# Plain TensorE products that nobody reads, in the score stage and the norms of a decoder layer

## The reference

```python
q, k, v = heads(x @ Wq), heads(x @ Wk), heads(x @ Wv)
attn = softmax(q @ k.T / sqrt(D))
...
x = layernorm(x + ((1 - blend) * attn @ v + blend * splat_attention(q, k, v)) @ Wo)
...
x_dbl = einsum('ke,bel->bkl', x_proj_w, u)
delta = softplus(einsum('er,brl->bel', dt_proj_w, dt_lo) + dt_proj_b)
state = state * exp(d_t * A) + (d_t * u_t) * B_t      # 512 steps, 512 x 16 states
x = layernorm(x + (y * silu(x)))
...
gate, up = split(x @ ternary(w_gate_up))
x = layernorm(x + rms_norm(silu(gate) * up) @ ternary(w_proj))
```

## Time and profile before

| | |
|---|---|
| median of 3 runs | 1458.05 us (1455.8 to 1459.01) |
| the profiled execution | 1459.91 us, its span from first to last instruction 1458.2 us |
| mean granted TensorE clock | 0.872 of full speed |
| busy | PE 83%, DVE 83%, ACT 52%, POOL 11% |
| the chain that ended last | PE 40%, DVE 35%, issue 9%, ACT 4% |

### The profile page before, as it was taken

How to read it: one execution, slowest core, us unless ns; L and a number is a source line. 1 busy time by engine, 2 the same in 40 slices (tenths; PEclk the granted TensorE clock), 3 DMA queues, 4 the chain that set the end, 5 groups by cost and what they waited for, 6 DMA issues and landing times.

```text
span 1458.2 us, 14219 instructions
## 1 busy us (share of the span) xinstructions
PE 1212.7 (83%) x4693; PEld 556.5 (38%) x4698; DVE 1204.1 (83%) x1457; ACT 763.8 (52%) x1118; POOL 164.9 (11%) x211
## 2 busy tenths in 40 slices
PE   4563885788689989899899898889799898987996
PEld 3332322233245543333355443333355433323553
DVE  5878898889979998879889997889799998786223
ACT  6765543536367753537477653455677545352331
POOL 1000111001101120100101121001111211001001
PEclk9875885889869999779889998799899998788998
DMA  6853796466329959553259686362389595540231
GB/s 196 286 170 116 169 248 165 102 145 145 59 87 244 253 133 265 132 129 87 67 135 271 165 226 192 87 166 52 89 220 269 120 255 133 135 104 15 65 102 44
DMA packets 112666, 220.20 MB, mean 151 GB/s; under 512 B 14560, under 2 KB 25312, under 8 KB 112592
## 3 DMA queue, kind: packets, MB, share of 16 engines
q1 hardware_dynamic: 88608, 142.85, 32.1%
q0 software_dynamic: 18432, 67.12, 23.9%
q10 hardware_dynamic: 5552, 9.31, 1.8%
HBM read 122.37 MB, written 29.62 MB: 104 GB/s over the span
## 4 chain that ended last, share of the span: by engine, by line
PE 40%; DVE 35%; issue 9%; ACT 4%; DMA 1%; DVEq 0%; POOL 0%; ACTq 0%; POOLq 0%
DVE ST L904 12%; PE ps L1382 6%; PE ps L1321 5%; PE ps L1514 5%; DVE MX L960 5%; PE ps L1304 5%; DVE ST L896 5%; PE ps L1458 3%; PE ps L1379 3%; PE ps L1414 3%; PE ps L1474 3%; DVE QAK L1130 2%; DVE QS L1117 2%; DMA YA<-ST 1%; DVE BST L940 1%
## 5 line engine op out<-in xcount | busy, mean ns | idle before, releaser
L904 DVE TENSOR_TENSOR_SCAN ST<-dA,ST 128x1024 f32<-128x1024 f32 x128 | 293.0, 2289 | 12.9 <-ACT dA L593 10.3
L1514 PE MATMUL ps<-V,GU 128*128 128x512 f16 x1024 | 239.9, 390 | 5.6 <-DVE V L1104 5.6
L960 DVE TENSOR_REDUCE MX<-ps 128x1 f32<-128x512 f32 x256 | 165.2, 686 | 76.3 <-PE ps L1304 76.0
L509 POOL DMA_DIRECT2D YA<-ST x128 | 109.3, 854 | 980.4 <-DVE ST L907 914.7
L593 ACT ACTIVATE dA<-DL,Aneg 128x511 f32<-128x511 f32 x256 | 168.3, 713 | 63.4 <-DVE ST L904 59.1
L731 ACT ACTIVATE PT<-ps 128x1024 f32<-128x1024 f32 x128 | 127.0, 1021 | 122.9 <-PE ps L1414 122.2
L1304 PE MATMUL ps<-KS,QS 96*128 96x512 f32 x256 | 129.4, 571 | 50.9 <-DVE MX L960 44.0
L907 DVE TENSOR_TENSOR ST<-ST,BC 128x1024 f32<-128x1024 f32 x128 | 156.8, 1225 | 4.4
L896 DVE TENSOR_TENSOR ST<-DU,BC 128x1024 f32<-128x1024 f32 x128 | 155.9, 1218 | 0.4 <-DMA YA<-ST 0.4
L1514 PEld LDWEIGHTS ps<-V,GU 128*128 128x128 bf16 x1024 | 97.4, 100 | 142.1 <-issue 33.0
L1474 PE MATMUL ps<-QS 128*128 128x512 f32 x512 | 142.1, 421 | 2.5 <-DVE QS L1117 1.6
(11 more groups left out here) (231 smaller groups left out, 1530.3 us busy)
## 6 DMA issues: line engine op xcount, KB each, us to landing
YA<-ST POOLq DMA_DIRECT2D x128, 512.0 KB, 7.3
BC<-bc_rows SPq DMA_DIRECT2D x64, 512.0 KB, 7.6
GU<-gu_tiles SPq DMA_DIRECT2D x64, 256.0 KB, 4.8
QS<-proj_tiles SPq DMA_DIRECT2D x64, 256.0 KB, 4.2
QS<-qk_parts SPq DMA_DIRECT2D x32, 256.0 KB, 4.2
KS<-qk_parts SPq DMA_DIRECT2D x32, 256.0 KB, 5.5
ST<-in_L_ffn_w_gate_up_dram SPq DMA_DIRECT2D x16, 256.0 KB, 3.7
gu_tiles<-BC SPq DMA_DIRECT2D x16, 256.0 KB, 2.1
```

What stands on the lines that cost most here:

```text
L904: nc.vector.tensor_tensor_scan(flat, dA[:, a, :, :].rearrange("p e s -> p (e s)"), flat, 0.0, ALU.mult, ALU.add).then_inc(s_scan, 1)
L960: nc.vector.tensor_reduce(MX[:, j % 2, qt, h:h + 1], ps[:, n % 2, :], AX_X, ALU.max).then_inc(s_mx, 1)
L1514: last = mm(ps[:, f % F_RING, :], GU[:, t % GU_RING, k, m * P:(m + 1) * P], XHL[:, z, k, :], start=(k == 0 and z == 0), stop=(k == KT - 1 ...
```

## The change

A new function `keep_busy(bank, times)` issues plain fp32 products of the identity matrix by one slice of `W`, into a PSUM bank whose content is not read any more. Nothing reads their results, and no semaphore is raised by them. The order of the instructions has 71 of them: 18 in each of batches 0 to 2, and 17 in the last.

- Score stage, ten a batch: one before and one behind the transposes of the first group's maxima; in group 1 three between the first two and the last two of the four `max_scores` that follow its first four L1414, and two behind the next pair of L1414; in group 2 three behind that same pair.
- Norms, eight a batch: one between `prep_xd` and `prep_dt` (not in the last batch), and 2, 1, 2 and 2 around the transposes of the second layernorm's rows.
- Each place has a wait that makes its bank free: for the last copies of Q and K out of bank 6 (`s_hi`), for the first or second exponential of the group (`s_exp`), for the last reads of the dt banks (`s_abs`, `s_rel`). That last wait stood behind the second tile of the feed-forward products before.

```diff
+            def keep_busy(bank, times):
+
+                for _ in range(times):
+                    mm(ps[:, bank, :], ident[:, :], W[:, 3, 0, :], start=True, stop=True)
...
                 max_scores(b, 0, 12, 16)
+                pe.wait_ge(s_hi, 2 * NG * (b + 1))
+                keep_busy(6, 1)
                 transpose_max(b, 0)
+                keep_busy(6, 1)
                 max_scores(b, 1, 0, X_AHEAD)
...
                             last.then_inc(s_s, 1)
+                            if j == 1 and kt == 0 and p == 1:
+                                max_scores(b, j + 1, 0, 2)
+                                pe.wait_ge(s_exp, 2 * KT * NG * b + 2 * KT * j + 1)
+                                keep_busy(score_bank(b, j, 0), 3)
+                                cuts[p] = 2
+                            if 0 < j < NG - 1 and kt == 1 and p == 0:
+                                pe.wait_ge(s_exp, 2 * KT * NG * b + 2 * KT * j + 2)
+                                keep_busy(score_bank(b, j, 2), 1 + j)
                             max_scores(b, j + 1, cuts[p], cuts[p + 1])
...
                     prep_xd(b + 1)
+                    keep_busy(7, 1)
                     for e in range(KT):
                         prep_dt(b + 1, e)
...
+                if not last_batch:
+                    pe.wait_ge(s_abs, KT * (b + 2))
+                    pe.wait_ge(s_rel, KT * (b + 2))
                 for r in range(KT):
+                    if r < KT - 1:
+                        keep_busy(7, (2, 1, 2)[r])
                     pe.wait_ge(s_lnx, 3 * KT * b + KT + r + 1)
...
+                keep_busy(7, 2)
                 pe.wait_ge(s_xl, KT * (b + 1))
...
-                    if t == 1 and not last_batch:
-                        pe.wait_ge(s_abs, KT * (b + 2))
-                        pe.wait_ge(s_rel, KT * (b + 2))
```

## The result

The changed kernel takes 1444.98 us (median of 4 runs, 1444.05 to 1445.55), the one before 1458.53 in the same comparison (4 runs, 1455.8 to 1459.31). The ratio is 0.9908, with a 95% interval of 0.9895 to 0.9921: 13.5 us less. I had forecast 1429, 29 us less. The profiled execution took 1444.05 us, with a span of 1442.3; its mean granted clock is 0.912, where it was 0.872.

A forecast was written before the change was run, and what follows sets the result against it. Taken as bound: neither TensorE nor DVE alone, TensorE's half clock making DVE wait. Of 42.3 us if all held, B and C 20.3, A 5.2, D 6.2 make 31.7; less a tenth, 28.5: 1429 us, range 1415 to 1450.

The forecast's parts named there:

- B: Score stage, group 1: clock held saves 13.6 us over batches 1 to 3; nine tenths taken, with C 20.3.
- C: Score stage, group 2: clock held saves 9.0 us over batches 1 to 3; nine tenths taken, with B 20.3.
- half of it holds: Rival, 27%: in each batch one or two places fall to half clock all the same; about 14 us gained, 1444.
- A: Around the transposes of the first group's maxima: 3.5 us a batch if held, 10.5 in three; half taken, 5.2.
- Windows at 0.50 shrink to one or none: Sign: half-clock stretches in batches 1 to 3 shrink from four a batch to one or none.
- mean clock above 0.92: Sign: TensorE's mean clock over the kernel rises from 0.872 to above 0.92.
- D: Norms, with the dt products and the gate and up products behind: 8.2 us if held; three quarters taken, 6.2.
- the case in which D gives little: If transposes don't count as work for the clock, D gives 6.2 us less: 1436; some 5 in a hundred.
- The 1.0 that I had counted for the dt products: In D: batch 1's dt products take 4.67 us against 3.69 in batch 2, so 1.0 to gain.
- Where a stretch gets faster other waits appear: a tenth off: Deduction over the whole sum for new waits, such as for ACT's exponentials: 31.7 us becomes 28.5.
- the overshoots: Products outlast their waits and delay work: 0.2 us in A, 1.2 in B, 0.6 in C, at most 0.5 in D.
- the slower rival: Rival, 9%: clock falls in or ahead of the products, each then takes 1.87 us; 24 us in four batches, 1482.

The follow-up runs named there:

- no_products: Changed kernel with every product taken out, the new order and waits kept; 1459.46 us, ratio 1.0006 to the kernel before.
- a_behind: Changed kernel plus a third product in A, behind the four max_scores, in the wait for the bias row; 1433.73 us, ratio 0.9823 to the kernel before.
- a_three_only: Kernel before plus only A's three products, the third behind the four max_scores; 1445.12 us, ratio 0.9918.
- few_rows: Changed kernel with all products working on 16 of the array's 128 rows; 1503.7 us, ratio 1.0302 to the kernel before.
- only_a: Kernel before plus only A's two products, at the first group's transposes; 1451.56 us, ratio 0.9947.
- all_again: Changed kernel run once more, unaltered; 1444.44 us, ratio 0.9884 to the kernel before.
- only_d: Kernel before plus only the products of the norms (D) with their waits; 1455.83 us, ratio 0.9973.
- only_bc: Kernel before plus only the products of groups 1 and 2 (B and C), with their waits and moved max_scores; 1452.74 us, ratio 0.9962.

## Why the prediction was right in its sign and wrong in its size

The mechanism is the one of the prediction: nothing but the products changes the time (`no_products` 1.0006), they do it through the clock (mean 0.872 to 0.912), and B and C of batches 1 to 3 have no stretch at 0.50 left. The time that came is that of the rival "half of it holds", 1444, but its reason, that one or two places a batch fall all the same, holds for A and the dt products alone. A accounts for 5 of the 13 us between forecast and result in the profiled pair; that the number fits is in part luck. "Windows at 0.50 shrink to one or none" and "mean clock above 0.92" did not come true. The step that failed is the price that the sum put on a stretch at half clock in B and C; two smaller ones failed with it.

- **A, taken at half, 5.2.** In the profiled execution it gave 0.2, in the runs 2.7 to 6.8. I had named the wait for the bias row as a reason for doubt and still counted half, where the step from "a wait is left" to "it falls there" was the right one. Held, the place is worth 3.0 us a batch (`a_behind`, `a_three_only`), near the 3.5 that I had worked out.
- **B and C, taken at 20.3.** They held, and gave 12.8 against the trace before and 6.2 against that of `no_products`. One mis-sized term is what stays of DVE's waits at full clock: I let 0.7 stay in B and 1.3 in C of batch 1, and 2.3 stayed in B beside the overshoot and 3.1 in C altogether. I had read the whole wait as the price of the clock; a good part is the turn in TensorE's queue. The other is the 7.0 us of wait in B of batches 2 and 3, worth 10.2 of the sum: I took it from one execution, and in `no_products`, with nothing to hold the clock, it is 3.9 and 4.0 (3.8 in batch 2 of `a_three_only`, which has the order of before).
- **D, taken at 6.2, and what comes behind.** The gate and up products gave 8.5, all of the 2.0 a batch that I had counted; so the case in which D gives little did not come. The 1.0 that I had counted for the dt products did not come either: the clock falls earlier in them, and they take 4.84 instead of 4.67. "Where a stretch gets faster other waits appear: a tenth off" did not cover what other sections lost, and it was meant for waits and not for the clock. The sections that got longer are those around the dt products (+0.5, +1.2), batch 0 ahead of the gate and up products (+1.4) and behind them (+1.3), the ends of batches 1 and 2 (+1.6, +0.3) and the one before A in batch 3 (+1.6). With the gain of 1.4 before the norms of batch 3 set against it, that is 6.5 of 22.4 us. In most of them the clock was at 0.50 for longer. Not in batch 0 ahead of the gate and up products: from 150 us to its YA transposes the granted clock rose from 0.82 to 0.86, and these transposes still started 1.7 us later. `no_products` has +4.9 before A in the three batches and the same -1.4 before the norms of batch 3, so shifts of this kind come without products too.

What was right: the overshoots, 1.2 us in B (1.17 measured); the moved waits at nothing (`no_products`); no new wait of DVE over 2 us; the slower rival's mechanism, by `few_rows`. Its size was not: its items for D add up to 9.2 and stood at 6, and the whole came to 44 us and not 24.

One rule that I had weighed is settled for this kernel. The Trainium skill, "TensorE: Matmul & The Clock Gate", section "Why this matters for your kernels", ties a drop to long idle gaps between bursts. Here the clock falls in A behind waits of 0.55 and 0.78 us, and one product in the second of them keeps it at 1.00 (`a_behind`), so the measurement decides against the rule as a test of where a fall can come. Part 1 of the page says that the point of the rise varies from run to run of one kernel. Only one execution of `only_a` was profiled, so no run here shows that this makes the 9 us between its runs.

Open: which execution has the stretch before A of batch 3 at 0.50 and which not, what places the falls of batch 0, why B and C without products come out so differently from trace to trace, and whether A's two products alone are worth 2.7 or 6.8 us.

## What to carry to other kernels

Idle gaps of under a microsecond in TensorE can cost several microseconds of half clock behind them, and a product that nobody reads, with all 128 rows, placed in the last of these gaps before the fall buys them back; find that gap in the timeline, since one product a batch there (`a_behind` against `all_again`, 10.7 us) did more than the sixteen a batch of B, C and D alone (5.6 and 2.6). Keep the filler short enough that its end is not waited for, and don't fill with products of few rows. When a gain is worked out from a half-clock stretch, first subtract what the other engine would wait at full clock too, and don't take the stretch's length from one execution: run the new order without the products, and compare with its trace as well.

## What I had not expected of the hardware

- The clock follows the rows of the array that are in use and not the engine's busy time alone. Sixteen-row products let it fall with TensorE occupied throughout (`few_rows`), and the four dt products kept it over 128 rows, of which 112 held zeros, where the same four over 16 rows lost it in nearly every batch.
- At 0.50, `max_scores` and L1422 with 96 and 97 rows kept TensorE busy 9.85 of 10.00 us (590 to 600 of the changed kernel) without raising the clock; the same instructions at 1.00 did not lose it once the gap was filled.
- Executions of one kernel can spread more once some of its gaps are filled: 6.1 us for the kernel before (23 runs), 9.2 for `only_a` (6), 10.4 for `only_d` (12); it was 4.1 for `only_bc` (6). The profile of one execution shows where the clock can fall, not how much a place is worth.
